# Last attention of a four-layer graph network: POOL's gathers start behind PE's products of the edge terms' masks

## The reference

```python
    z = h @ W_fc.T
    z_src = z[src]
    z_dst = z[dst]
    ex = e @ W_edge.T
    wm = [W_m1, W_m2]
    src_m = _moments(z_src, wm)
    dst_m = _moments(z_dst, wm)
    ...
    a = z_src @ blk[0] + z_dst @ blk[K] + ex @ w_e
    for k in range(1, K):
        a = a + src_m[k] @ blk[k] + dst_m[k] @ blk[K + k]
    att = jnp.where(a > 0, a, SLOPE * a)
    m = jax.ops.segment_max(att, dst, num_segments=N)
    expv = jnp.exp(att - m[dst])
    denom = jax.ops.segment_sum(expv, dst, num_segments=N)
    w = expv / denom[dst]
    ez = ex @ W_e2n.T
    msg = w[:, None] * (z_src + ez)
    return jax.ops.segment_sum(msg, dst, num_segments=N)
```

## Time and profile before

| | us |
|---|---|
| median of three timed runs | 1912.07 (1908.1 to 1912.09) |
| profiled execution, first to last instruction | 2674.2 |
| POOL busy | 1227.4 (46%) |
| PE busy | 1501.4 (56%) |
| DVE busy | 1423.4 (53%) |
| ACT busy | 1008.8 (38%) |
| first attention, first gather to last sum | 51.8 to 1470.1 |
| last attention, first gather to the loop's last sum | 1818.4 to 2640.3 |

### The profile page before, as it was taken

One profiled execution on the slowest core, in us unless ns is written; L12 is line 12 of the kernel. 1 busy time (PEld: TensorE's weight loads), 2 busy tenths in 40 slices (PEclk: granted clock), 3 DMA queues, 4 the chain that ended last, 5 costly groups with the idle time before them and its releaser, 6 DMA issues. The chain is left out here.

```text
span 2674.2 us, 43621 instructions
## 1 busy us (share of the span) xinstructions
PE 1501.4 (56%) x12903; PEld 1250.3 (47%) x12903; DVE 1423.4 (53%) x3785; ACT 1008.8 (38%) x2221; POOL 1227.4 (46%) x1328
## 2 busy tenths in 40 slices
PE   3555555555555654555555774754134656555795
PEld 2444444434444443344434673753033645444785
DVE  6455555555555554555555787871023534434685
ACT  3333333333333333333333651750003534434683
POOL 2555555555555554545553460546724343444100
PEclk7677777777777767777777787885556777777897
DMA  5222222222222222222221210022201111111100
GB/s 116 54 58 56 58 59 57 59 57 61 57 58 60 56 59 52 60 55 58 59 57 35 62 59 3 2 87 34 35 17 33 37 34 37 32 41 33 40 26 14
DMA packets 125233, 128.69 MB, mean 48 GB/s; under 512 B 80959, under 2 KB 88435, under 8 KB 124840
## 3 DMA queue, kind: packets, MB, share of 16 engines
q0 software_dynamic: 35776, 62.74, 10.4%
q1 hardware_dynamic: 63778, 57.41, 7.8%
q10 hardware_dynamic: 25542, 6.81, 1.1%
HBM read 116.64 MB, written 10.20 MB: 47 GB/s over the span
## 5 line engine op out<-in xcount | busy, mean ns | idle before, releaser
L634 POOL DMA_INDIRECT shared<-kv_tab,idx x784 | 763.2, 974 | 674.3 <-DMA idx<-in_src 459.3
L836 PE MATMUL bank<-key_hot,lo_hot 128*128 128x350 f16 x784 | 220.8, 394 | 586.5 <-DVE count L698 392.4
L836 PEld LDWEIGHTS bank<-key_hot,lo_hot 128*128 128x128 f16 x784 | 59.3, 101 | 703.4 <-issue 690.4
L2282 POOL DMA_INDIRECT count<-att_tab,count x240 | 228.3, 951 | 301.7 <-PE bank L2827 193.4
L698 DVE TENSOR_TENSOR count<-count,bank 128x350 f32 x392 | 205.4, 524 | 109.4 <-issue 73.6
L735 DVE TENSOR_TENSOR acc<-acc,bank 65x64 f32 x98 | 21.3, 217 | 429.2 <-remote 425.8
L779 ACT ACTIVATE expo<-score 128x32 f32<-128x32 f32 x98 | 22.5, 229 | 587.3 <-DVE score L716 566.9
L769 ACT ACTIVATE lo_dist<-iota_neg,tile_lo 128x128 f16<-128x128 f32 x784 | 238.5, 389 | 0.0
L2656 ACT ACTIVATE shared<-shared 128x126 f32<-128x126 bf16 x336 | 144.4, 484 | 172.0 <-PE bank L2804 88.6
L683 DVE TENSOR_SCALAR key_hot<-iota_key,tile_key 128x350 f16<-128x350 f16 x784 | 193.3, 319 | 0.0
L851 PEld LDWEIGHTS bank<-hots,msg 128*65 128x65 f32 x1568 | 183.8, 221 | 0.4 <-DVE msg L725 0.4
(11 more groups left out here) (528 smaller groups left out, 3237.8 us busy)
## 6 DMA issues: line engine op xcount, KB each, us to landing
shared<-in_edge_attr SPq DMA_DIRECT2D x97, 256.0 KB
shared<-lo_tab SPq DMA_DIRECT2D x28, 512.0 KB
shared<-kv_tab,idx POOLq DMA_INDIRECT x784
count<-att_tab,count POOLq DMA_INDIRECT x240
qwin<-q_tab ACTq DMA_DIRECT2D x196, 16.0 KB
kv_tab<-count SPq DMA_DIRECT2D x1, 1600.0 KB, 10.4
idx<-in_src SPq DMA_DIRECT2D x97, 4.0 KB, 1.6
g_edge<-att_tab,count POOLq DMA_INDIRECT x94
```

Of the source, the lines that this page charges most:

```text
L634: nc.gpsimd.indirect_dma_start(kv[:, s, c, :], None, kv_tab, bass.IndirectOffsetOnAxis(ap=idx[:, s, c:c + 1], axis=0)).then_inc(kv_in[s], 16)
L836: last = nc.tensor.matmul(bank[6 + q % 2][:, 0:KC], lo_hot[:, c, :], key_hot[:, c, :], start=i == 0, stop=i == GT - 1)
L2282: nc.gpsimd.indirect_dma_start(ring[s][:, j, 0:D + 2], None, att_tab[1], bass.IndirectOffsetOnAxis(ap=src_i[:, t:t + 1], axis=0)).then_inc ...
```

## The change

POOL gets one more wait ahead of its first gather of the last attention. Before, it waits for the list of sources (`src_in`) and for the stored table (`table_in`); now also for PE's signal `turned_v`, which PE raises to 2 when its 42 products of the edge terms' masks are done. Nothing else differs.

```diff
             def _(pool):
                 pool.wait_ge(src_in, 16)
                 pool.wait_ge(table_in, 16)
+                pool.wait_ge(turned_v, 2)
                 for i in range(NPU):
                     s = i % SLOTS
                     if i >= SLOTS:
```

## The result

The median went from 1911.46 us to **1938.53 us** (four runs each): slower by 27 us. The ratio estimated from all runs is lower than that of the medians, 1.0115 with a 95% interval of 1.008 to 1.015, which is 15 to 29 us; one of the four runs with the change took only 1924.99 us. The forecast was 1938.

What follows compares the result with a forecast made beforehand. The prediction took POOL's gather spacing, 1.25 us a gather, as the bound, so POOL's whole delay of 26 us is lost: 1912.07 + 26 = 1938 us, range 1905 to 1952.

Steps and rivals of the forecast that it cites:

- POOL's spacing paces the timed runs: Both attentions' gather loops: in timed runs they go at POOL's spacing, 1.25 us a gather.
- the sum of the parts: Whole kernel: the least the timed runs must contain, 1885.8 us, leaving 26.3 us of the timed median and no room for the freeze.
- no change: Rival 2, last attention: POOL is not the bound in timed runs; 1912 to 1916 us, chance 0.10.
- DVE would be 22 us ahead of POOL at unit 20: Last attention before the change: DVE needs unit 20 at 397 us after the table, POOL lands it at 419.5.
- X = 26 us: POOL's delay at the last attention, from table to PE's signal: 26 us, between 22.5 and 37.6.
- The wait for unit 1, 14 us: DVE's loop after the change: unit 1 lands 42 us after the signal, wanted at 28.3, a new 14 us wait.
- rival 3: The 42 masks: they would take up to 12 us from early gathers; +14 instead of +26, 1926 us, chance 0.05.
- The recorded span after stays at 2674 us, with a freeze in the first iterations: Recording after the change: span 2674 us within some 40, the freeze moved into the last attention's first iterations.
- the freeze belongs to the recorded execution: Last attention: gathers and computing nearly exclude each other from 1823 to 1959 us only in the recording, not in timed runs.
- faster: Rival 1, the 42 mask products: the freeze is in timed runs too and the wait frees that stretch; chance 0.16.

Runs made afterwards that it cites:

- the second recording of before: The kernel without the change, not edited, recorded once more: span 1909.9 us, time 1911.92 us (one execution).
- the frozen recording: The first recording of the kernel without the change, shown ahead of the prediction: span 2674.2 us, where the median of the three timed runs was 1912.07.
- 30 dense units: ND 30 instead of 28, so 302 gathers: without the change 1904.46 us against 1911.79 for the kernel before, with the change 1925.96.
- 29 dense units: The kernel without the change, ND 29 instead of 28, so 318 gathers instead of 334: 1892.81 us against 1912.72.
- four kernels that delay the gathers: The change (1938.53 us), waits on 18 mask products (1921.86) or on DVE's first loop arguments (1948.36) instead, and the change with 30 dense units (1925.96).
- half the delay: The kernel with the change, but POOL waits for 18 of the 42 mask products instead of all: 1921.86 us against 1912.72 for the kernel before.

## Why the prediction was right, point by point

- *POOL's spacing paces the timed runs*: right, and the step that everything hung on. It came from the sum of the parts against the timed median, where the recorded span would have led to "no change". Two recordings that last as long as the timed runs now show the loops directly: 334 gathers at 1.30 us each before, 1.285 after, where the earlier trace rows had 1.25. That the sum came so close was partly luck. In the second recording of before the 784 gathers took 24.5 us more than the 980, the last attention up to unit 20 took 16.1 more than the 419.5, and the stretch from the last of the 784 to the last sum 7.5 us instead of the 26.0, which came from the frozen recording. With 0.4 us between the attentions, 1.6 at the end and 2 outside the span, these make up the 26 us that the sum had left open.
- *DVE would be 22 us ahead of POOL at unit 20*: the second recording of before has 20.2 us of waits for gathered rows in all. The difference is right, its two sides are not: counted from the first gather, unit 20 was used at 435.6 us, where 419.5 was forecast for POOL, and DVE's path without the waits was 415.4, where 397 was forecast. The term that was too small is the loop: 25 iterations took 363 us without the waits, not the 343 that came from the end of the frozen recording, where no gathers ran beside them. The two errors cancel.
- *X = 26 us*: the signal came 29.9 us later than the first gather did before, counted from the store. A little over, as PE got a lower clock than the 0.80 taken: masks and powers took 22.8 us at a granted clock of 0.65, where 18.9 was forecast. In the second recording of before they took 18.7 us at 0.81. So some 4 us of the delay, by this estimate, come from the clock and not from the place of the signal in the program.
- *The wait for unit 1, 14 us*: 15.45.
- *Gathers are not stretched by DVE's masks* (rival 3): wrong in the direction, and small. The durations of the earlier trace rows come from the frozen recording, where masks and gathers hardly met. In the second recording three of the first twelve gathers took 2.35, 2.22 and 1.73 us instead of 0.95, 3.45 us in all, one of them across the first 14 masks. The Trainium skill ("SBUF — State Buffer", "Who interferes with whom") says that an instruction of VectorE in a two-port mode can block GpSimd: the trace agrees with its direction, with 3.5 us instead of the 12 that I drew from it. Only the first of the three lies beside masks alone, so the lock as the cause is argued, not shown.
- *The recorded span after stays at 2674 us, with a freeze in the first iterations*: wrong. The step that failed is "the freeze belongs to the recorded execution" as a rule for every recording. All later recordings, with gathers beside the masks or not, have the length of the timed runs. Of the rule in the Trainium skill that the block for trace records pushes back on its producers inside ("NOTIFIC — the notification-queue block", section "7.1 Overflow: three behaviours, one of which stalls the engine") no run here shows that it caused the freeze: the same program was recorded twice more without one. What froze the first recording stays open; no run here brings it back.
- *The rivals*: faster and no change did not come. That the start of the gathers costs less where they are not the bound was tried with 30 dense units: 20.0 instead of 25.4 us by the rows of the recordings; the medians, 21.5 and 27, lie within the noise of each other.

## What to carry to other kernels

Before pricing rows of a recording that is much longer than the timed runs, add up what the timed runs must contain at least, by the spacing of the slowest serial stream; here that left 26 of 1912 us and named the bound, though one term, read from the frozen recording, was 18.5 us too large. A stream with a fixed cost per item can be the bound even where its engine is busy for only 65% of the span, and where it is, a wait put at its head is paid nearly in full (here 0.7 to 0.9 us for each us); whether it is the bound can be tried by moving one unit of its work elsewhere, which here also gave a faster kernel (29 dense units, 1893 us).

## What the runs showed that was not expected

The powers and the last masks, the same instructions on PE, ran slower in all four kernels that delay the gathers, one recording of each. 50 powers took 8.40, 8.43, 8.40 and 8.51 us there, and 5.71, 5.66, 5.71 and 5.83 us in the four recordings with gathers beside them (the freeze left aside); the last 24 mask passes 5.58 us against 4.42 to 4.59. In the kernel with the change:

```profile
1423.25 9.15 PE L2749 MATMUL bank<-ident,shared 128*128 128x128 f32 x60
1432.24 8.40 PE L2754 MATMUL bank<-deg,count 128*128 128x2 f32 x50
1440.50 5.58 PE L2749 MATMUL bank<-ident,shared 128*128 128x128 f32 x24
```

Stretches of 5 us each (columns as in the earlier trace rows), in the kernel with the change:

```profile
1429.00:1434.00 5.00, 5.00 (x48) 5.00 (x46) 4.92 (x20) 0.61 (x1) 0.00 (x0) 1.00 0.36 111
1434.00:1439.00 5.00, 5.00 (x28) 5.00 (x28) 0.97 (x3) 0.00 (x0) 0.00 (x0) 0.57 0.33 105
1439.00:1444.00 5.00, 5.00 (x23) 4.78 (x24) 0.16 (x1) 0.00 (x0) 0.00 (x0) 0.50 0.00 0
```

and in the second recording of before:

```profile
1424.00:1429.00 5.00, 5.00 (x48) 5.00 (x47) 4.92 (x20) 0.73 (x1) 4.21 (x3) 1.00 0.44 132
1429.00:1434.00 5.00, 5.00 (x40) 5.00 (x40) 1.26 (x5) 0.00 (x0) 3.89 (x4) 0.84 0.41 125
1434.00:1439.00 5.00, 3.45 (x21) 3.04 (x20) 1.06 (x8) 0.00 (x0) 3.78 (x5) 0.82 0.16 27
```

PE had worked nearly without a gap in both (in the last stretch of the second its masks end at 1437.07). In the first the granted clock falls from 1.00 to 0.50, the lower level, during the powers; in the second it stays above 0.8. This makes up most of the 4.4 us by which the loop begins later with the change. Gathers beside the powers are not by themselves what keeps it up: with half the delay they had begun, and the powers took 8.43 us. Why the clock falls sooner in the delayed kernels was not tried and stays open.
